# Last stage: ScalarE writes two of the input norms as scale times x plus shift

## The chip, the cores and the metric

One Trainium2 chip, one core of it. The time is the device time of the whole program in microseconds, the median of several runs. The core has four compute engines that each run their own instruction stream in order: TensorE (PE; its weight loads are shown as PEld), VectorE (DVE), ScalarE (ACT) and GpSimd (POOL). SyncE (SP) issues transfers. They wait for each other through semaphores.

## The reference, cut to what matters

A chain of four layers over x of 8 sequences x 256 tokens x 128 features, each layer a token mixer and a feed-forward part, each with a norm ahead and one behind. Only the last layer matters here. Its mixer's scores are over channels (b, k, q), its feed-forward part routes each token to two of eight experts by its distance to their centroids.

```python
def _layernorm(x, axis=-1, eps=1e-05):
    m = jnp.mean(x, axis=axis, keepdims=True)
    v = jnp.var(x, axis=axis, keepdims=True)
    return (x - m) / jnp.sqrt(v + eps)
...
x = x + _layernorm(_L3_attn_ref(_layernorm(x, axis=-1), L3_attn_Wq, L3_attn_Wk, L3_attn_Wv, L3_attn_Wo), axis=-1)
x = x + _layernorm(_L3_ffn_ref(_layernorm(x, axis=-1), L3_ffn_centroid, L3_ffn_Wg, L3_ffn_bg, L3_ffn_W1, L3_ffn_b1, L3_ffn_W2, L3_ffn_b2), axis=-1)
```

The change is in how the two inner `_layernorm(x)` of these two lines are written: the one ahead of the mixer and the one ahead of the router and experts.

## The kernel before

The last stage is one call of `experts` with `by_distance` true. x lies in SBUF as 16 tiles of 128 tokens by 128 features; a run is four tiles (two sequences), so there are four runs, 0 to 3. Both parts of the layer are in the same stage: its opening does mixer and router for the four runs, interleaved, then come the expert blocks (slots, in pairs of gate/up and down matmuls) and a tail with the last norm.

`mixed_events` is one list of events, written by hand. Every engine walks the same list and does its own part of each event, in order, with no reordering; an engine that must wait at one event does nothing of a later one. Step k of the list takes, with a = k, b = k-1, c = k-2, d = k-3: `c_shift c`, `c_res c`, `c_scores b`, `c_proj a`, `stats c`, `one_hot d`, `c_zn b`, `gap d`, `norm c`, then spot and share of d (the ranks of the chosen experts and the row places), the sends, `c_stats a+1`, `c_out b`, `router c`, `c_norm a+1`, `score c`. The events that start with c_ are the mixer's.

What each engine does at the events around the change:

- `c_norm r` (mixer's input norm). VectorE: `channel_norm`, four writes by `centred` (L1810) into `cy`, (x - mean) * rstd, after GpSimd's power operation (L1714) made rstd. TensorE: fillers, then four transposes (L2412). ScalarE: one copy of them to `cyT` (L2188).
- `c_proj r`. TensorE: q/k (L2274) and v (L2279). ScalarE: copies (L2191, L2196).
- `c_scores r`. TensorE: scores (L2293). VectorE: adds the block mask and takes the maximum (L1837 on). ScalarE: Exp.
- `c_zn r`. VectorE scales the weights, TensorE multiplies by v (L2305), ScalarE copies (L2209).
- `c_out r`. TensorE: output projection (L2313). VectorE: its statistics (L1798).
- `c_shift r`, `c_res r`. VectorE makes a shift (L1857), ScalarE writes the output norm as scale times projection plus shift (`normed`, L2145), VectorE adds it to x (L2083).
- `norm r` (the router's input norm). VectorE: four writes by `centred` into `yrow` (L1810). TensorE: fillers, four transposes (L2435). ScalarE: copy to `yT` (L2219), then a second copy of the rows (L2222).
- `router r`, `score r`. TensorE: the products with the centroids (L2446). VectorE: distances, the two best experts.
- `gap r`: Exp on ScalarE (L2228). `spot r`: TensorE ranks the choices (L2329, L2334).

Between these, the experts' weights are cut into high and low parts: VectorE subtracts the last row (L1815), ScalarE writes the high part (L2137 to L2139), VectorE the low part (L1822 to L1824). `keep_busy` puts filler matmuls (L2267) into TensorE's queue, a fixed number at each place; TensorE runs through them before it takes up what follows. The router's rows go to DRAM by GpSimd's indirect transfers (L1726), four tiles x two copies a run, and the expert blocks are loaded from there. The first slot comes after the ranks of run 3.

Of the kernel before, what the change touches and what calls it, by code (L numbers as in the profile page):

```python
# [14 lines left out]
ALU = mybir.AluOpType  # L15
# [3 lines left out]
P = 128  # L19
# [3 lines left out]
TILES = SEQS * T  # L23
# [12 lines left out]
RT = 4  # L36
# [1478 lines left out]
def experts(nc, g, layer, key, w, mix=None, out=None):  # L1515
# [8 lines left out]
    by_distance = layer == 3  # L1524
# [8 lines left out]
    x = g.x  # L1533
    rows, acc = g.rows[layer], g.acc[layer]
    with ExitStack() as ctx:
        st = Stage(nc, ctx, f"m{layer}")
# [47 lines left out]
        if by_distance:  # L1584
            cat = columns(g.w[mix], MIX)
            dist = [st.sb(f"dist{k}", [P, RT, 2]) for k in range(2)]
            shares = st.sb("shares", [P, 2, RT])
            sq_y = st.sb("sq_y", [P, TILES])
            ones_f = st.sb("ones_f", [P, P])
            c2 = st.sb("c2", [P, 3 * NE])  # L1590
            flat = [p[:, :, :, :].rearrange("p k t d -> p (k t d)") for p in parts]
            cqk = [p.rearrange("p (t c) -> p t c", t=RT) for p in flat[0:2]]
            cvT = [flat[2][:, k * RUN:(k + 1) * RUN] for k in range(2)]
            cy, cyT = flat[3][:, 0:RUN], flat[3][:, RUN:2 * RUN]
            ccT, cf = (st.sb(n, [P, RUN]) for n in ("ccT", "cf"))
            cz, cz_exp, czn = (st.sb(n, [P, 2, P]) for n in ("cz", "cz_exp", "czn"))
            ctop, cneg, ctotal, crecip = (st.sb(n, [P, 2]) for n in ("ctop", "cneg", "ctotal", "crecip"))
            cshift = st.sb("cshift", [P, TILES])

        loaded = g.loaded[key]  # L1600
        (tables_ready, places_ready, region_ready, hi_ready, split_ready, in_var, in_rstd, y_ready, copied, yT_ps,
# [14 lines left out]
        result_sent = [st.sem(f"result_sent{k}") for k in range(RB)]  # L1616
        parts_loaded = [st.sem(f"parts_loaded{r}") for r in range(RUNS)]
        if by_distance:
            dist_ready, c2_ready, c2_ps, less_ready, stored = (st.sem(n) for n in (
                "dist_ready", "c2_ready", "c2_ps", "less_ready", "stored"))  # L1620
            (c_in_var, c_in_rstd, c_y_ready, c_yT_ps, c_yT_ready, c_qk_ps, c_qk_ready, c_v_ps, c_v_ready, c_z_ps,
             c_top_ready, c_exp_ready, c_zn_ready, c_cx_ps, c_cx_ready, c_out_ps, c_out_var, c_out_rstd, c_shift_ready,
             c_f_ready, c_x_done) = (st.sem(n) for n in (
                 "c_in_var", "c_in_rstd", "c_y_ready", "c_yT_ps", "c_yT_ready", "c_qk_ps", "c_qk_ready", "c_v_ps",
                 "c_v_ready", "c_z_ps", "c_top_ready", "c_exp_ready", "c_zn_ready", "c_cx_ps", "c_cx_ready", "c_out_ps",
                 "c_out_var", "c_out_rstd", "c_shift_ready", "c_f_ready", "c_x_done"))
# [39 lines left out]
        def tiles(r):  # L1666
            return slice(r * RT, r * RT + RT)
# [100 lines left out]
        def _(dve):  # L1768
# [39 lines left out]
            def centred(k, j, r, o):  # L1808
                t = r * RT + j
                return nc.vector.tensor_scalar(o, x[:, t, :], mv[k][:, t, 0:1], rstd[k][:, t:t + 1], ALU.subtract, ALU.mult)  # L1810
# [6 lines left out]
            def split(e):  # L1817
# [6 lines left out]
                nc.vector.tensor_tensor(down[0:r, 2, 1, :], raw_rest, down[0:r, 2, 0, :].bitcast(F32),  # L1824
                                        ALU.subtract).then_inc(split_ready, 1)

            def channel_norm(r):
                dve.wait_ge(c_in_rstd, r + 1)
                if r >= 1:
                    dve.wait_ge(c_yT_ps, r)  # L1830
                for j in range(RT):
                    last = centred("c_in", j, r, cy[:, j * P:(j + 1) * P])
                last.then_inc(c_y_ready, 1)

            def channel_scores(r):
                dve.wait_ge(c_z_ps, r + 1)
# [15 lines left out]
                    last = nc.vector.tensor_scalar(czn[:, s, :], cz_exp[:, s, :], crecip[:, s:s + 1], None, ALU.mult)  # L1852
                last.then_inc(c_zn_ready, 1)

            def shifts(k, r, o, ready, done):
                dve.wait_ge(ready, r + 1)
                nc.vector.scalar_tensor_tensor(o[:, tiles(r)], mv[k][:, tiles(r), 0], -1.0, rstd[k][:, tiles(r)],  # L1857
                                               ALU.mult, ALU.mult).then_inc(done, 1)

            def norm(r):  # L1860
                dve.wait_ge(in_rstd, r + 1)
                for j in range(RT):
                    last = centred("in", j, r, yrow[0][:, r * RT + j, 0:P])
                last.then_inc(y_ready, 1)
# [263 lines left out]
        def _(act):  # L2128
# [53 lines left out]

            for kind, r, *_ in events:
                if kind == "c_norm":
                    act.wait_ge(c_yT_ps, r + 1)
                    if r >= 1:
                        act.wait_ge(c_v_ps, r)
                    nc.scalar.activation(cyT[:, :], ps[:, 0, :], ACT.Copy).then_inc(c_yT_ready, 1)  # L2188
# [21 lines left out]
                if kind == "c_shift":  # L2210
                    if r >= 1:
                        act.wait_ge(c_x_done, r)
                    normed(r, c_shift_ready, c_f_ready, lambda j: cf[:, j * P:(j + 1) * P],
                           lambda j: ps[:, 6, j * P:(j + 1) * P], "c_out", cshift)
                if kind == "norm":
                    act.wait_ge(yT_ps, r + 1)
                    if r >= 2:
                        act.wait_ge(router_ps, r - 1)
                    nc.scalar.activation(yT[r % 2][:, :], ps[:, 7, :], ACT.Copy).then_inc(yT_ready, 1)  # L2219
                    act.wait_ge(y_ready, r + 1)  # L2220
                    n = P - 1 if by_distance else P
                    nc.scalar.activation(yrow[1][:, tiles(r), 0:n], yrow[0][:, tiles(r), 0:n], ACT.Copy).then_inc(copied, 1)  # L2222
# [1368 lines left out]
```

## Time and profile before

| what | value |
|---|---|
| median of 3 runs | 1065.38 us (1065.27 to 1066.95) |
| the profiled execution | 1067.32 us |
| its span, first to last instruction | 1065.6 us |
| mean granted TensorE clock | 0.957 |
| PE busy | 941.6 us (88%) |
| DVE busy | 731.4 us (69%) |
| ACT busy | 561.7 us (53%) |
| POOL busy | 471.6 us (44%) |
| the opening of the last stage | 860 to 945 us |
| its first expert slot | 951.3 us |

The shares are means over stages with different limits. A row of the timeline gives the start, the length, the engine, the line, the operation with the names it writes and reads, how many instructions were merged, and in square brackets the idle time of the engine just before and what ended it. m_parts holds the mixer's `cy` and `cyT` among others, m_yrow the router's rows, m_banks all of PSUM.

### The profile page before, as it was taken

Reading aid. Unit: us, or ns where it says so; the run is one execution under the profiler, and the core shown is the slowest. Engines: PE = TensorE matmul, PEld = TensorE weight load, DVE = VectorE, ACT = ScalarE, POOL = GpSimd, SP = SyncE. Lnnn points to the kernel's source line nnn. Section 1 sums busy time; section 2 is a strip of 40 time slices with the busy share of each in tenths; the row PEclk is TensorE's granted clock in tenths of the full one; section 3 lists DMA queues with packets and bytes.
Section 4 is the critical chain, followed back from the end, with each engine's and each line's share of the span. In section 5 each row is a group of like instructions: output and inputs, shape, how many; then the busy total and the mean of one; then the engine's idle time right before and its main releaser. Section 6 shows DMA issues by size and latency. Waiting matters only on the chain. (4 is left out here: it accounts for less than half of the span.)

```text
span 1065.6 us, 24404 instructions
## 1 busy us (share of the span) xinstructions
PE 941.6 (88%) x8310; PEld 740.4 (69%) x8310; DVE 731.4 (69%) x2014; ACT 561.7 (53%) x1168; POOL 471.6 (44%) x528
## 2 busy tenths in 40 slices
PE   7999987999994799999979999999999968869990
PEld 6666665889993676665666666777666857869990
DVE  4677754676665678888567567676577778866664
ACT  2567673246663467777536555544445435326662
POOL 2366655464345222232454333343456432685442
PEclk9999999899997899999989999999999988999995
DMA  9211120022113024222210011110111720022214
GB/s 307 63 55 54 56 66 11 25 73 67 40 49 88 1 63 132 73 69 73 71 31 2 3 42 42 42 41 3 42 42 42 273 71 1 27 66 72 61 39 118
DMA packets 80739, 66.47 MB, mean 62 GB/s; under 512 B 6690, under 2 KB 73425, under 8 KB 80235
## 3 DMA queue, kind: packets, MB, share of 16 engines
q1 hardware_dynamic: 71883, 54.34, 18.2%
q0 software_dynamic: 4512, 8.47, 2.4%
q10 hardware_dynamic: 4224, 2.10, 0.8%
q8 instruction: 71, 1.16, 0.5%
q14 instruction: 49, 0.40, 0.1%
HBM read 38.76 MB, written 26.58 MB: 61 GB/s over the span
## 5 line engine op out<-in xcount | busy, mean ns | idle before, releaser
L780 DVE TENSOR_REDUCE a_rowmax<-a_banks 128x4 f32<-128x1024 f32 (+1 forms) x112 | 136.9, 1223 | 49.9 <-PE a_banks L1147 19.7
L2662 POOL TENSOR_TENSOR a_both<-a_probs 128x512 f32<-128x512 f32 x64 | 86.5, 1351 | 141.7 <-ACT a_probs L2964 141.6
L964 ACT ACTIVATE a_probs<-a_banks 128x1024 f32<-128x1024 f32 x112 | 114.8, 1025 | 53.8 <-PE a_banks L1128 42.6
L1733 POOL DMA_INDIRECT acc<-m_result,m_yb x77 | 75.4, 980 | 89.6 <-DVE m_result L2045 49.8
L2964 ACT ACTIVATE a_probs<-a_banks 128x1024 f32<-128x1024 f32 x64 | 65.5, 1023 | 85.5 <-PE a_banks L3136 85.5
L2818 DVE TENSOR_REDUCE a_rowmax<-a_banks 128x4 f32<-128x1024 f32 x64 | 77.7, 1220 | 12.5 <-PE a_banks L3109 12.5
L1726 POOL DMA_INDIRECT rows<-m_yrow,m_idx x64 | 65.3, 1020 | 38.5 <-issue 18.6
L2158 ACT ACTIVATE m_gate<-m_banks 128x352 f32<-128x352 f32 (+1 forms) x93 | 42.8, 460 | 65.9 <-PE m_banks L2364 65.9
L3152 PE MATMUL a_banks<-a_probs,a_V 128*64 128x256 f32 x512 | 69.4, 392 | 0.0
L655 POOL TENSOR_SCALAR_AFFINE_SELECT a_probs<-a_probs 128x512 f32<-128x512 f32 (+1 forms) x48 | 37.9, 790 | 63.3 <-ACT a_probs L964 63.2
L2390 PE MATMUL m_banks<-e_down,m_hT_hi 128*128 (+2 forms) x231 | 64.2, 346 | 0.6 <-DVE m_hT_lo L2028 0.6
L1170 PE MATMUL a_banks<-a_probs,a_V 128*32 128x256 f32 x720 | 58.0, 394 | 0.5 <-POOL a_probs L655 0.4
L2267 PE MATMUL m_banks<-ident 128*128 128x128 f32 x362 | 52.6, 308 | 2.4 <-DVE m_score L1881 1.5
L2362 PE MATMUL m_banks<-e_gu_hi,m_y_hi 128*128 x154 | 53.9, 350 | 0.4 <-issue 0.4
L1128 PE MATMUL a_banks<-a_QT,a_KT 25*128 25x256 f32 x384 | 48.1, 325 | 6.5 <-DVE a_rowmax L780 5.2
L2028 DVE TENSOR_TENSOR m_hT_lo<-m_banks,m_hT_hi 128x384 fp32r<-128x384 f32 x93 | 51.1, 549 | 3.6 <-ACT m_hT_hi L2164 3.6
L2022 DVE TENSOR_TENSOR m_h<-m_banks,m_gate 128x342 f32<-128x342 f32 (+1 forms) x55 | 28.5, 518 | 36.2 <-ACT m_gate L2158 36.2
L2267 PEld LDWEIGHTS m_banks<-ident 128*128 128x128 f32 x362 | 50.0, 221 | 4.0 <-issue 2.8
L2391 PE MATMUL m_banks<-e_down,m_hT_lo 128*128 (+2 forms) x231 | 51.7, 224 | 0.0
L2364 PE MATMUL m_banks<-e_gu_hi,m_y_lo 128*128 x154 | 49.7, 323 | 0.0
L2375 PE MATMUL m_banks<-ident,m_h 128*128 128x128 f32 (+2 forms) x279 | 47.3, 279 | 2.7 <-DVE m_hT_lo L2028 2.3
L2363 PE MATMUL m_banks<-e_gu_lo,m_y_hi 128*128 x154 | 49.5, 321 | 0.0
(403 smaller groups left out, 2764.5 us busy)
## 6 DMA issues: line engine op xcount, KB each, us to landing
rows<-fill SPq DMA_DIRECT2D x16, 520.0 KB, 4.3
a_factor<-recip_rows SPq DMA_DIRECT2D x28, 256.0 KB, 4.7
rows<-fill SPq DMA_DIRECT2D x15, 455.0 KB, 3.9
m_yb<-rows SPq DMA_DIRECT2D x77, 65.0 KB
a_expert<-in_experts SPq DMA_DIRECT2D x16, 257.5 KB
e_gu_lo<-in_gu SPq DMA_DIRECT2D x1, 2736.0 KB
e_last_row<-in_last_rows SPq DMA_DIRECT2D x1, 2736.0 KB
e_gu_lo<-in_gu SPq DMA_DIRECT2D x1, 2464.0 KB, 12.0
```

Of the source, the lines that this page charges most:

```text
L780: nc.vector.reduce_max(o, src, AX).then_inc(rowmax_ready, 1)
L964: nc.scalar.activation(probs[h][:, k, :, :], ps[:, 4:6, :], ACT.Exp, scale=SCALE).then_inc(exp_done, 1)
L1170: last = mm(o[:, 0:SEQ], v, probs[h][:, b // 2 + (0 if causal else 2 * kt), jj, (b % 2) * SEQ:(b % 2 + 1) * SEQ], start=kt == 0, stop=kt = ...
L1726: nc.gpsimd.indirect_dma_start(rows.rearrange("n p c -> (n p) c"), bass.IndirectOffsetOnAxis(idx[:, c:c + 1], 0), yrow[k][:, r * RT + t, : ...
L1733: nc.gpsimd.indirect_dma_start(acc.rearrange("k n d -> (k n) d"), bass.IndirectOffsetOnAxis(yb[b % YB][:, P:P + 1].bitcast(U32), 0), resul ...
L2267: mm(ps[:, b, 0:P], g.ident[:, :], g.ident[:, :], start=True, stop=True)
L2362: mm(o, y_hi[i % 3][:, :], gu_hi[:, s], start=True, stop=False)
L2390: mm(both, hT_hi[i % 2][0:r, c, :], part[0:r, c, :, :], start=c == 0, stop=False)
L2662: nc.gpsimd.tensor_tensor(both[u % 4][:, :, :], p[:, :, 0, :], p[:, :, 1, :], ALU.add).then_inc(both_ready, 1)
L2818: nc.vector.reduce_max(rowmax[i % 2][:, :, j, :, n].rearrange("p t h -> p h t"), ps[:, b:b + 2, :].rearrange("p h (t k) -> p h t k", t=T), ...
L2964: nc.scalar.activation(probs[u % 4][:, :, :, :].rearrange("p h t q -> p h (t q)"), ps[:, 4:6, :], ACT.Exp, scale=SCALE).then_inc(exp_done, 1)
L3152: last = mm(ps[h * D64:(h + 1) * D64, 6, 0:SEQ], V[i % 3][:, kt, j, :], probs[b][:, h, kt, :], start=kt == 0, stop=kt == T - 1)
```

## The change

In the last stage alone, VectorE no longer writes the two input norms. For each run it makes one shift per token, minus mean times rstd (`shifts`, one operation over 128 x 4), and ScalarE writes the four tiles as rstd * x + shift with `normed`. ScalarE does this at the same event of the list, ahead of its copy of the transposes, and so behind all that stands before that event in its own order. The transposes wait for ScalarE's write in place of VectorE's. The first stage with the same code (`by_distance` false) keeps its norm on VectorE.

```diff
--- before.py
+++ after.py
@@ -1595,7 +1595,7 @@
             ccT, cf = (st.sb(n, [P, RUN]) for n in ("ccT", "cf"))
             cz, cz_exp, czn = (st.sb(n, [P, 2, P]) for n in ("cz", "cz_exp", "czn"))
             ctop, cneg, ctotal, crecip = (st.sb(n, [P, 2]) for n in ("ctop", "cneg", "ctotal", "crecip"))
-            cshift = st.sb("cshift", [P, TILES])
+            cshift, c_in_shift, in_shift = (st.sb(n, [P, TILES]) for n in ("cshift", "c_in_shift", "in_shift"))
 
         loaded = g.loaded[key]
         (tables_ready, places_ready, region_ready, hi_ready, split_ready, in_var, in_rstd, y_ready, copied, yT_ps,
@@ -1616,6 +1616,7 @@
         result_sent = [st.sem(f"result_sent{k}") for k in range(RB)]
         parts_loaded = [st.sem(f"parts_loaded{r}") for r in range(RUNS)]
         if by_distance:
+            c_in_shift_ready, in_shift_ready = st.sem("c_in_shift_ready"), st.sem("in_shift_ready")
             dist_ready, c2_ready, c2_ps, less_ready, stored = (st.sem(n) for n in (
                 "dist_ready", "c2_ready", "c2_ps", "less_ready", "stored"))
             (c_in_var, c_in_rstd, c_y_ready, c_yT_ps, c_yT_ready, c_qk_ps, c_qk_ready, c_v_ps, c_v_ready, c_z_ps,
@@ -1824,13 +1825,13 @@
                 nc.vector.tensor_tensor(down[0:r, 2, 1, :], raw_rest, down[0:r, 2, 0, :].bitcast(F32),
                                         ALU.subtract).then_inc(split_ready, 1)
 
+            def shifts(k, r, o, ready, done):
+                dve.wait_ge(ready, r + 1)
+                nc.vector.scalar_tensor_tensor(o[:, tiles(r)], mv[k][:, tiles(r), 0], -1.0, rstd[k][:, tiles(r)],
+                                               ALU.mult, ALU.mult).then_inc(done, 1)
+
             def channel_norm(r):
-                dve.wait_ge(c_in_rstd, r + 1)
-                if r >= 1:
-                    dve.wait_ge(c_yT_ps, r)
-                for j in range(RT):
-                    last = centred("c_in", j, r, cy[:, j * P:(j + 1) * P])
-                last.then_inc(c_y_ready, 1)
+                shifts("c_in", r, c_in_shift, c_in_rstd, c_in_shift_ready)
 
             def channel_scores(r):
                 dve.wait_ge(c_z_ps, r + 1)
@@ -1852,12 +1853,10 @@
                     last = nc.vector.tensor_scalar(czn[:, s, :], cz_exp[:, s, :], crecip[:, s:s + 1], None, ALU.mult)
                 last.then_inc(c_zn_ready, 1)
 
-            def shifts(k, r, o, ready, done):
-                dve.wait_ge(ready, r + 1)
-                nc.vector.scalar_tensor_tensor(o[:, tiles(r)], mv[k][:, tiles(r), 0], -1.0, rstd[k][:, tiles(r)],
-                                               ALU.mult, ALU.mult).then_inc(done, 1)
-
             def norm(r):
+                if by_distance:
+                    shifts("in", r, in_shift, in_rstd, in_shift_ready)
+                    return
                 dve.wait_ge(in_rstd, r + 1)
                 for j in range(RT):
                     last = centred("in", j, r, yrow[0][:, r * RT + j, 0:P])
@@ -2182,6 +2181,10 @@
 
             for kind, r, *_ in events:
                 if kind == "c_norm":
+                    if r >= 1:
+                        act.wait_ge(c_yT_ps, r)
+                    normed(r, c_in_shift_ready, c_y_ready, lambda j: cy[:, j * P:(j + 1) * P],
+                           lambda j: x[:, r * RT + j, :], "c_in", c_in_shift)
                     act.wait_ge(c_yT_ps, r + 1)
                     if r >= 1:
                         act.wait_ge(c_v_ps, r)
@@ -2213,6 +2216,9 @@
                     normed(r, c_shift_ready, c_f_ready, lambda j: cf[:, j * P:(j + 1) * P],
                            lambda j: ps[:, 6, j * P:(j + 1) * P], "c_out", cshift)
                 if kind == "norm":
+                    if by_distance:
+                        normed(r, in_shift_ready, y_ready, lambda j: yrow[0][:, r * RT + j, 0:P],
+                               lambda j: x[:, r * RT + j, :], "in", in_shift)
                     act.wait_ge(yT_ps, r + 1)
                     if r >= 2:
                         act.wait_ge(router_ps, r - 1)
```

## Rows read from the trace of the kernel before

**Rows 1.** Busy us by stretch: PE, PEld, DVE, ACT, POOL (instructions), clock, DMA.
```profile
860.00:945.00 85.00, 67.27 (x443) 60.22 (x444) 67.92 (x333) 35.20 (x84) 40.34 (x38) 0.89 0.05 17
```

**Rows 2.** Groups by shape, VectorE, 860 to 945 us: busy, mean ns.
```profile
L1810 DVE TENSOR_SCALAR m_yrow<-x,m_in_mv,m_in_rstd 128x128 f32<-128x128 f32 x16 | 4.7, 354 | 3.9 <-POOL m_in_rstd L1714 3.9
...
L1810 DVE TENSOR_SCALAR m_parts<-x,m_c_in_mv,m_c_in_rstd 128x128 f32<-128x128 f32 x16 | 4.5, 344 | 0.9 <-POOL m_c_in_rstd L1714 0.9
```

**Rows 3.** Timeline (start us, us, engine, line): ScalarE's norm; its hand-over.
```profile
1057.73 3.31 ACT L2145 ACTIVATE m_parts<-m_parts,m_shift,m_out_rstd 128x128 f32<-128x128 f32 x8 [1.26 <-DVE m_shift L1857]
...
914.42 0.16 DVE L1857 SCALAR_TENSOR_TENSOR m_cshift<-m_c_out_mv,m_c_out_rstd 128x4 f32<-128x4 f32 x1
...
914.68 1.51 ACT L2145 ACTIVATE m_cf<-m_banks,m_cshift,m_c_out_rstd 128x128 f32<-128x128 f32 x4 [3.93 <-DVE m_cshift L1857]
```

**Rows 4.** Timeline: mixer's norm, runs 0 and 1.
```profile
865.08 1.11 DVE L1810 TENSOR_SCALAR m_parts<-x,m_c_in_mv,m_c_in_rstd 128x128 f32<-128x128 f32 x4
...
866.11 0.17 DVE L1784 CAST m_limit_f<-m_limit 128x16 f32<-128x16 int32 x1
...
866.25 0.66 PE L2412 MATMUL m_banks<-ident,m_parts 128*128 128x128 f32 x4 [0.57 <-DVE m_parts L1810]
...
869.01 0.77 ACT L2137 ACTIVATE e_gu_hi<-e_gu_lo 128x684 fp32r<-128x684 f32 x1 [0.31 <-DVE e_gu_lo L1815]
...
871.07 0.63 PE L2412 MATMUL m_banks<-ident,m_parts 128*128 128x128 f32 x4 [0.63 <-DVE m_parts L1810]
...
871.10 0.58 ACT L2196 ACTIVATE m_parts<-m_banks 128x512 f32<-128x512 f32 x1
...
871.53 1.06 PE L2293 MATMUL m_banks<-m_parts 128*128 128x128 f32 x8
...
874.25 0.41 DVE L1837 TENSOR_TENSOR m_cz<-m_banks,late_w_att 128x256 f32<-128x256 f32 x1
```

**Rows 5.** Timeline: mixer's norm, run 2.
```profile
882.34 1.12 DVE L1810 TENSOR_SCALAR m_parts<-x,m_c_in_mv,m_c_in_rstd 128x128 f32<-128x128 f32 x4
...
883.51 0.66 PE L2412 MATMUL m_banks<-ident,m_parts 128*128 128x128 f32 x4
...
886.30 0.68 DVE L2083 TENSOR_TENSOR x<-x,m_cf 128x512 f32<-128x512 f32 x1
```

**Rows 6.** Timeline: router's norm, run 0.
```profile
892.18 0.60 ACT L2209 ACTIVATE m_ccT<-m_banks 128x512 f32<-128x512 f32 x1 [1.78 <-PE m_banks L2305]
...
892.44 0.95 PE L2435 MATMUL m_banks<-ident,m_yrow 128*128 128x128 f32 x4 [0.29 <-DVE m_yrow L1810]
...
893.18 1.92 PE L2313 MATMUL m_banks<-late_w_att,m_ccT 128*128 128x128 f32 x8
...
895.13 0.89 DVE L1798 BATCH_NORM_STATS2 m_c_out_stats<-m_banks 128x6 f32<-128x128 f32 x4 [1.24 <-PE m_banks L2313]
```

**Rows 7.** Timeline: TensorE's fillers and VectorE's norm, mixer, run 3.
```profile
896.45 2.91 PE L2267 MATMUL m_banks<-ident 128*128 128x128 f32 x12
...
896.67 1.12 DVE L1810 TENSOR_SCALAR m_parts<-x,m_c_in_mv,m_c_in_rstd 128x128 f32<-128x128 f32 x4
```

**Rows 8.** Timeline: router's norm, run 1.
```profile
907.79 0.60 ACT L2209 ACTIVATE m_ccT<-m_banks 128x512 f32<-128x512 f32 x1 [1.70 <-PE m_banks L2305]
...
907.82 0.63 PE L2435 MATMUL m_banks<-ident,m_yrow 128*128 128x128 f32 x4
...
908.29 0.20 ACT L2228 ACTIVATE m_th<-m_gap 128x4 f32<-128x4 f32 x1
...
908.49 1.14 PE L2313 MATMUL m_banks<-late_w_att,m_ccT 128*128 128x128 f32 x8
```

**Rows 9.** Timeline: router's norm, run 2.
```profile
924.91 0.66 PE L2435 MATMUL m_banks<-ident,m_yrow 128*128 128x128 f32 x4 [0.38 <-DVE m_yrow L1810]
```

**Rows 10.** Timeline: TensorE behind the router's norm, run 3.
```profile
943.84 3.82 PE L2267 MATMUL m_banks<-ident 128*128 128x128 f32 x32
...
948.00 0.20 PE L2329 MATMUL m_banks<-m_one_hot,m_upper 128*128 128x64 bf16 x1 [0.34 <-DVE m_chosen L1924]
```


## Prediction

> **What bounds the kernel now.** I read the profile in four steps. First the page: its 40 slices show a full TensorE with short dips, and the last dips before the long expert run lie where the last stage opens. Second, busy time by stretch, for the opening of that stage, 860 to 945 us [rows 1]: of 85.0 us VectorE is busy 67.9, TensorE 67.3 (much of it the filler of keep_busy), ScalarE 35.2, GpSimd 40.3. VectorE is the fullest engine and ScalarE is 60% idle, so the change looks obvious. But 68 of 85 is not full, and a share doesn't say who is late at a given wait. Third, the chain that ended last: it reaches back only into the last quarter of it, so for most of the stretch it gives no answer. So, fourth, the timeline, hand-over by hand-over. It shows a ring: VectorE writes a norm, TensorE turns it, ScalarE copies it, TensorE multiplies, VectorE reads. Every engine takes its events in one fixed order, and each of them waits somewhere in each step. For instance VectorE stood idle for 1.24 us until the output projection (L2313) of run 1 was done [rows 6]. In such a ring, latency on the path counts and engine time beside it does not.
>
> After 945 us TensorE is nearly full until the last expert block, and the tail is untouched. What the opening loses or gains therefore arrives at the end one for one.
>
> **What the change removes and adds.** Removed on VectorE: 8 groups of four writes, 16 for the mixer at 344 ns and 16 for the router at 354 ns [rows 2]. A group holds VectorE's queue for 1.03 us: it starts at 865.08 and the next operation, which waits for nothing, at 866.11 [rows 4]. Each group leaves one small operation like L1857's 0.16 us [rows 3]; as the next one can start before it ends (866.11 is 0.08 ahead of 865.08 + 1.11), it holds the queue for about 0.08. VectorE is relieved of about 0.95 us each time, 7.6 in all.
>
> Added on ScalarE: 8 groups of four. The same function already writes SBUF from SBUF in the tail, eight in 3.31 us, so 1.66 for four [rows 3]. All 8 together are 13.3 us on an engine with 50 us free. No table load is added: the stage already uses this function beside Exp.
>
> Added on the path: the hand-over. Before, from the first VectorE write to the first transpose took 1.17 us (865.08 to 866.25 [rows 4], 882.34 to 883.51 [rows 5]). After: start of the shift to start of ScalarE's group 0.26 us (914.42 to 914.68, the same pair of operations), the group 1.66, and about 0.05 to TensorE: 1.97. **So each hand-over is 0.80 us longer even when ScalarE stands free.** Where it isn't free, the group stands behind what ScalarE has ahead of it in its order, and that was not so before, because VectorE wrote beside it.
>
> **The eight places, in order of time** (each number is how much later the thing named starts than before; the page's own clock levels are kept).
>
> Mixer, run 0: ScalarE is free. First transpose 866.25 becomes 867.05, +0.80 [rows 4].
>
> Mixer, run 1: ScalarE's order puts two weight conversions, the q/k copy and the v copy ahead. Before, conversion 1 idled 0.31 us for VectorE [rows 4]; VectorE is now 0.95 early there, so this gives back 0.4 of the 0.8: the 0.31 and the 0.1 by which ScalarE's operations overlap when none waits (907.79 + 0.60 is 908.39, the next starts at 908.29 [rows 8]). The q/k copy moves by that 0.4, the v copy from 871.10 to 871.5, and the group can start behind its 0.58 us, at 872.0, only. It ends at 873.7, so the transposes go from 871.07 to 873.7, +2.65. The score matmuls follow 0.46 later and take 1.06 (from 871.53): done at 875.25. VectorE read them at 874.25, because it was busy till then; now it waits and reads at 875.3. **Of 2.65 the cover swallows 1.6; +1.05 stays.**
>
> Mixer, run 2: VectorE's writes at 882.34 lay under a wait for GpSimd's power operation, so removing them gains nothing. ScalarE is free. The transposes move by 1.05 + 0.80 = 1.85 (883.51), and with them the copy, the output norm and VectorE's residual add at 886.30 [rows 5], which had almost no slack: **+1.8**.
>
> Router, run 0: on ScalarE the group stands behind the copy of L2209, which itself waits for TensorE: 892.18 + 1.8 = 894.0, 0.60 long [rows 6]. Group 894.5 to 896.2. Transposes from 892.44 to 896.2: **+3.8**. In TensorE's order the output projection (L2313) stands behind these transposes, and VectorE was already idle for it (895.13 [rows 6]); so VectorE is late by 3.8 too. This is the added wait that costs most: queued behind it on TensorE are the projection and the router, on VectorE the output statistics and everything after.
>
> Mixer, run 3: TensorE runs 12 filler matmuls before these transposes, 2.91 us from 896.45 [rows 7]. Shifted by 3.8 they end at 903.2. VectorE's write stood 1.54 behind the start of the statistics (895.13 to 896.67 [rows 6, 7]), so the shift comes at 898.9 + 1.5 = 900.4 and the group ends at 902.4. Hidden: +0. Without the filler it would cost up to its 2 us.
>
> Router, run 1: the same as run 0, with the Exp of the gap ahead too. L2209's copy 907.79 + 3.8 = 911.6, Exp 908.29 + 3.8 = 912.1 (0.20 long); group 912.2 to 913.9. Transposes 907.82 to 913.9: **+6.1** [rows 8]. The ranks, the projection and the router follow on TensorE, and GpSimd's sends follow on VectorE's shares.
>
> Router, run 2: ScalarE is free, +0.80: the transposes at 924.91 [rows 9] are late by **+6.9**, and the ranks right behind them. VectorE reads those as soon as they are done.
>
> Router, run 3: again +0.80, so +7.7. Behind them TensorE has 32 fillers, 943.84 + 7.7 + 3.82 = 955.4, and only then the ranks, which began at 948.00 after 0.34 us of waiting for VectorE [rows 10]: **+7.4**. VectorE's one-hots are ready by then.
>
> The sum, as what each place adds to the lateness (run 0 of the mixer is inside run 1's figure, and at the last place the fillers swallow 0.3 of 0.8): 1.05 + 0.75 + 2.0 + 0 + 2.3 + 0.8 + 0.5 = 7.4 us. It hangs on the order of ScalarE's queue at two places (4.3 of it) and on the hand-over at the others.
>
> **TensorE's clock.** It is the one price that the trace brackets only. The projection of L2313 takes 1.92 us while the granted clock is at the lower of its two levels, 1.2 GHz (893.18) [rows 6], and 1.14 at the higher, 2.4 (908.49) [rows 8], 0.78 apart. New TensorE waits of over 2 us arise before the transposes of mixer run 1 and router runs 0 and 1; at router run 0 the clock is low already. Bounds: nothing, or one more fall at both others, with transposes, projection and ranks slow and some filler running over the next wait, about 3. Below nothing is excluded, since the waits only grow. I take 0.4, half of one projection, nearer to nothing because filler and waits further on absorb part. The Trainium skill (Perfetto Trace Analysis, Matmul Optimizations) says that TensorE scales power by utilization, so matmuls should run back to back in batches; by it alone the upper end would hold and the time be about 1076.
>
> **Against the runs.** The profiled execution took 1067.3 us, of which its span is 1065.6; the median of the runs is 1065.4, 1.9 below it. The difference is carried over: 1065.4 + 7.4 + 0.4 = 1073.2 us, and a profile after with a span near 1073.4.
>
> **The rivals.**
> VectorE is the bound: the opening shrinks by all that VectorE is relieved of, 8 x 0.95 = 7.6, to 1057.8. It decides if at each step VectorE, not TensorE, is the last to arrive; it speaks for it that VectorE has the largest share, against it the 1.24 us wait at 895.13 and that the cost moves to an engine standing on the same ring. The Trainium skill (Perfetto Trace Analysis, Optimizing Scalar/DVE Operations) says that offloading from VectorE to ScalarE may make sense if VectorE is saturated; at 68 of 85 us the trace doesn't show it saturated. Chance 0.04.
> Both cancel: every hand-over costs 0.80 but VectorE's 0.95 is paid back before the next read, and ScalarE reaches each group in time. 8 x (0.80 - 0.95) = -1.2, so 1064.2, no difference. It needs ScalarE's copy at 892.18 to be early, and the trace shows it waiting for TensorE. Chance 0.05.
> The clock falls at both new waits: +3 instead of +0.4, 1075.8. Chance 0.14.
> That the change doesn't do what it says: VectorE's eight groups would still be in the trace; nothing in the diff leaves them. Under 0.01.
>
> **How the numbers follow.** The forecast has 0.77, and 1073.2 is its value. Its own range is 1069 (the two queue places cost half, because ScalarE gets through faster or VectorE's lead helps an earlier read) to 1076. With the clock rival the range is 1069 to 1077; it leaves out the two rivals on the other side and the ends, under 2 in 10. A measurement of this kernel can tell about 0.2%, 2.1 us, from no change: faster 0.04, same 0.05, slower 0.91.
>
> **What would show it.** In the profile after, the transposes of L2435's router run 0 start about 3.8 us later, run 1 about 6.1, and ScalarE's new groups start right behind the copy of L2209. VectorE's idle before the output statistics of run 1 rises from 1.24 to over 4 us. The first expert slot begins 7 to 8 us later, and from there to the end nothing changes. VectorE's busy time in the stretch falls to about 60 us, ScalarE's rises to about 48. It would be wrong if the read at 874.25 or at 895.13 didn't move, or if VectorE's waits didn't grow.

## The result and the profile after

The kernel with the change took 1076.94 us in the median of 6 runs (1073.71 to 1089.31), the kernel before beside it 1066.04. The ratio is 1.0121, 95% interval 1.0096 to 1.0147: some 13 us slower, where 7.8 were forecast. The sign and the place were right, the size was too small. The median as it stands lies inside the range of 1069 to 1077, near its end; scaled to the median of before from which the forecast was made (1065.38) it is 1078.3, just above it. Executions that took over 1.5% longer than the fastest of the same kernel are left out of every ratio here.

The page after, busy time by engine (before: PE 941.6, DVE 731.4, ACT 561.7):

```profile
PE 942.7 (88%) x8310; PEld 741.7 (69%) x8310; DVE 723.7 (68%) x1990; ACT 575.2 (54%) x1200; POOL 470.3 (44%) x528
```

VectorE lost 7.7 us of work and ScalarE gained 13.5, as summed (7.6 and 13.3). The page says nothing of the loss: the shares moved as intended.

The profiled execution after took 1073.71 us with a span of 1072.0, only 6.4 more than before. That hides a chance difference: its last stage began 5.4 us earlier, in code that the change doesn't touch. So from here on I count from a mark inside the stage, VectorE's first subtraction of a last row (L1815 before, 864.29; L1816 after, 858.88), and call the time from there to the first gate matmul of the first slot the opening. It is this row before and this row after (from, length, then busy time of PE, PEld, DVE, ACT, POOL, then the granted clock):

```profile
864.29:951.34 87.05, 68.93 (x478) 61.18 (x477) 69.52 (x344) 34.47 (x85) 43.88 (x38) 0.92 0.07 20
```

```profile
858.88:957.49 98.61, 74.44 (x479) 65.94 (x478) 61.97 (x320) 47.47 (x117) 44.22 (x39) 0.84 0.07 19
```

87.05 us became 98.61, 11.6 more. From the first slot to the end both took the same (114.3 and 114.5), so the whole loss is in the opening, and the granted clock there fell from 0.92 to 0.84.

The timeline after, at the places of the prediction (start us, length us, engine, line; in brackets the idle time ahead and what ended it):

```profile
858.88 0.87 DVE L1816 TENSOR_TENSOR e_gu_lo<-e_gu_lo,e_last_row 128x684 f32<-128x684 f32 x1 [1.02 <-DMA e_down<-in_down]
...
859.66 0.16 DVE L1830 SCALAR_TENSOR_TENSOR m_c_in_shift<-m_c_in_mv,m_c_in_rstd 128x4 f32<-128x4 f32 x1
...
859.86 1.65 ACT L2144 ACTIVATE m_parts<-x,m_c_in_shift,m_c_in_rstd 128x128 f32<-128x128 f32 x4 [3.79 <-DVE m_c_in_shift L1830]
...
861.56 0.66 PE L2418 MATMUL m_banks<-ident,m_parts 128*128 128x128 f32 x4 [1.18 <-ACT m_parts L2144]
...
862.90 3.19 PE L2280 MATMUL m_banks<-late_w_att,m_parts 128*128 128x256 f32 x8 [0.69 <-ACT m_parts L2191]
...
869.75 0.63 PE L2418 MATMUL m_banks<-ident,m_parts 128*128 128x128 f32 x4 [2.31 <-ACT m_parts L2144]
...
872.02 0.42 DVE L1838 TENSOR_TENSOR m_cz<-m_banks,late_w_att 128x256 f32<-128x256 f32 x1 [4.48 <-PE m_banks L2299]
...
881.75 0.65 PE L2418 MATMUL m_banks<-ident,m_parts 128*128 128x128 f32 x4 [1.73 <-ACT m_parts L2144]
...
889.45 0.16 DVE L1830 SCALAR_TENSOR_TENSOR m_in_shift<-m_in_mv,m_in_rstd 128x4 f32<-128x4 f32 x1 [0.31 <-POOL m_in_rstd L1715]
...
890.37 0.60 ACT L2212 ACTIVATE m_ccT<-m_banks 128x512 f32<-128x512 f32 x1 [1.78 <-PE m_banks L2311]
...
890.86 1.64 ACT L2144 ACTIVATE m_yrow<-x,m_in_shift,m_in_rstd 128x128 f32<-128x128 f32 x4
...
892.55 1.12 PE L2441 MATMUL m_banks<-ident,m_yrow 128*128 128x128 f32 x4 [2.22 <-ACT m_yrow L2144]
...
893.46 1.92 PE L2319 MATMUL m_banks<-late_w_att,m_ccT 128*128 128x128 f32 x8
...
895.41 0.89 DVE L1799 BATCH_NORM_STATS2 m_c_out_stats<-m_banks 128x6 f32<-128x128 f32 x4 [4.28 <-PE m_banks L2319]
...
908.66 0.60 ACT L2212 ACTIVATE m_ccT<-m_banks 128x512 f32<-128x512 f32 x1 [1.99 <-PE m_banks L2311]
...
909.25 1.64 ACT L2144 ACTIVATE m_yrow<-x,m_in_shift,m_in_rstd 128x128 f32<-128x128 f32 x4
...
911.03 1.09 PE L2441 MATMUL m_banks<-ident,m_yrow 128*128 128x128 f32 x4 [2.41 <-ACT m_yrow L2144]
...
946.52 0.66 PE L2441 MATMUL m_banks<-ident,m_yrow 128*128 128x128 f32 x4 [0.87 <-ACT m_yrow L2144]
...
948.78 5.44 PE L2273 MATMUL m_banks<-ident 128*128 128x128 f32 x32
...
957.49 0.42 PE L2368 MATMUL m_banks<-e_gu_hi,m_y_hi 128*128 x1 [0.51 <-issue]
```

Read it beside [rows 4] to [rows 10]. The hand-over at mixer run 0 is shift 859.66, group 859.86, 1.65 long, transposes 861.56: 1.90 us against 1.17. At router run 0 the shift is there at 889.45, but ScalarE takes L2212's copy (L2209 before) at 890.37 and the group only behind it at 890.86; TensorE idles 2.22 us for it, and VectorE idles 4.28 us ahead of the output statistics where it idled 1.24 [rows 6]. Run 1 repeats that (908.66, 909.25, 911.03). These are the mechanisms forecast. Not forecast are the lengths on TensorE. L2280 takes 3.19 at mixer run 0, where before, behind the same wait of 0.69, it was (L2274 there):

```profile
867.59 1.99 PE L2274 MATMUL m_banks<-late_w_att,m_parts 128*128 128x256 f32 x8 [0.69 <-ACT m_parts L2188]
```

The granted clock over these eight matmuls was 1.00 before and 0.60 after. And the 32 fillers of L2273 take 5.44 where they took 3.82 [rows 10], at 0.69 in place of 1.00.

All marks counted from the first subtraction, as lateness against the first profile of before, in us; "again" is a second profile of the changed kernel (e5, below), "before again" a second profile of the kernel before (e12, below):

| what starts | forecast | after | again | before again |
|---|---|---|---|---|
| mixer run 0, transposes | 0.80 | 0.72 | 0.71 | -0.01 |
| mixer run 1, transposes | 2.65 | 4.09 | 2.59 | 0.00 |
| VectorE's read of the scores, run 0 | 1.05 | 3.18 | 0.96 | 0.01 |
| mixer run 2, transposes | 1.85 | 3.65 | 0.96 | 0.15 |
| router run 0, transposes | 3.8 | 5.52 | 2.83 | 0.15 |
| output statistics, run 1 | 3.8 | 5.69 | 3.00 | 0.32 |
| router run 1, transposes | 6.1 | 8.62 | 6.04 | 0.19 |
| router run 2, transposes | 6.9 | 9.70 | 7.13 | 1.05 |
| router run 3, transposes | 7.7 | 10.34 | 7.78 | 1.86 |
| first slot | 7.4 | 11.55 | 11.14 | 1.35 |

The last column says how far a single profile can be trusted: the kernel before repeats itself within 0.35 us up to router run 1, and at router run 3 only within 1.9.

### The profile page after: what moved, and what is told of

Same layout as the page of the kernel before. It is cut to its first block and busy times, and to the rows that moved or that the text cites. A ratio compares the mean times of both kernels' runs of the same rounds, so it can differ in the third digit from the quotient of the medians.

```text
span 1072.0 us, 24412 instructions
## 1 busy us (share of the span) xinstructions
PE 942.7 (88%) x8310; PEld 741.7 (69%) x8310; DVE 723.7 (68%) x1990; ACT 575.2 (54%) x1200; POOL 470.3 (44%) x528
## 3 DMA queue, kind: packets, MB, share of 16 engines
q8 instruction: 71, 1.16, 0.5%
## 5 line engine op out<-in xcount | busy, mean ns | idle before, releaser
L1734 POOL DMA_INDIRECT acc<-m_result,m_yb x77 | 75.5, 980 | 91.3 <-DVE m_result L2044 49.8
L2273 PE MATMUL m_banks<-ident 128*128 128x128 f32 x362 | 51.6, 303 | 2.5 <-DVE m_score L1880 1.7
L2273 PEld LDWEIGHTS m_banks<-ident 128*128 128x128 f32 x362 | 48.7, 216 | 4.4 <-issue 3.2
L1092 PE MATMUL a_banks<-ident 128*128 128x128 f32 x298 | 43.0, 288 | 7.8 <-DMA w_att<-in_att 6.4
```

What stands on the lines that cost most here:

```text
L1734: nc.gpsimd.indirect_dma_start(acc.rearrange("k n d -> (k n) d"), bass.IndirectOffsetOnAxis(yb[b % YB][:, P:P + 1].bitcast(U32), 0), resul ...
L2273: mm(ps[:, b, 0:P], g.ident[:, :], g.ident[:, :], start=True, stop=True)
```

## The experiments

The first eight ran in two sessions (e1 to e4, then e5 to e8) in which every kernel took about 1100 us and scattered more (the kernel before 1099.6 and 1100.0 in the median); what is longer there lies mainly ahead of the last stage, whose opening began between 882 and 907 us. In the third session, e9 to e12, the kernel before took 1067.65. The record gives e1 to e4 and e9 to e12 the same chip number, so what made the first two slower is not known. I compare ratios to the kernel before in the same session, and marks inside the opening. One profile stands for one execution, and the clock is part luck, which is why e5 and e12 repeat the two kernels themselves. In four profiles of those two sessions (e1, e4, e5, e7) TensorE also idled 2.3 us between the transposes of the first two expert blocks, where the others show 0.69 (e8: 1.58, and 2.0 ahead of the first). e5 has it and the first profile after, the same kernel, has not, so it follows no edit; it puts about 2 us on the opening of these four, 1.6 of it at this place. Router run 3's transposes are the last mark ahead of it.

### One norm at a time

```diff
 # e1: the router's norm stays on VectorE
             def norm(r):
-                if by_distance:
-                    shifts("in", r, in_shift, in_rstd, in_shift_ready)
-                    return
 # e2: the mixer's norm stays on VectorE
             def channel_norm(r):
-                shifts("c_in", r, c_in_shift, c_in_rstd, c_in_shift_ready)
+                ... four writes by centred, as before
```

(and ScalarE's side of each goes with it)

> Only the mixer's input norm on ScalarE; the router's stays on VectorE. I read the opening of the last stage as the time from VectorE's first subtraction of a last row (L1815 before, L1816 after) to the first gate matmul of the first slot: before 951.34 - 864.29 = 87.05 us, after 957.49 - 858.88 = 98.61, 11.6 more. Theory path-and-clock (hand-overs 7.4 us as summed, the rest TensorE's lower clock): opening 89 to 91, that is 2 to 4 more, time 1067.5 to 1069.5. Rival clock-only (hand-overs are covered, TensorE's waits only push its clock down): most of the loss starts at mixer run 1, so 7 or more of the 11.6 should be here already, 1073 or above. Rival VectorE-bound: not slower at all, 1062 to 1065.

> Only the router's input norm on ScalarE. Theory path-and-clock: 2.0 + 2.3 + 0.8 + 0.5 = 5.6 us of hand-over and queue order plus 1 to 3 us of clock: opening 93.5 to 96, time 1072 to 1075, and the context copy (L2209 before) with the new group right behind it at router runs 0 and 1. Rival clock-only: the smaller part, under 1070. If both parts add up, this and the mixer's run give 11.6 together.

Measured: e1 1.0036 (0.9996 to 1.0077), opening 92.96; e2 1.0055 (1.0019 to 1.0091), opening 94.12. The ratios add up to 0.9%, and the changed kernel has 1.0 to 1.2%; each is known to about 0.4%, so this agrees but doesn't prove much. The openings, 5.9 and 7.1 more, add up to 13.0 against 11.6, and to 11.4 without the 1.6 us of that wait. The router's part is as expected in its opening (93.5 to 96) and just under in its time. The mixer's part is larger than expected by its opening, not by its ratio; at its own places it is as forecast (transposes of run 1 +2.59, read of the scores +0.96), and by router run 3 it is 3.1 late. Of its opening's 5.9, 2.8 arise behind that, 1.6 of them in the wait named above. Clock-only wanted 7 or more of the opening here and fails by it, and with it VectorE-bound, which wanted nothing; the ratio of e1 alone excludes neither.

### More fillers in the changed kernel

```diff
-                    keep_busy((9, 0, 8, 6)[r], 0)
+                    keep_busy((13, 8, 14, 6)[r], 0)
...
-                        keep_busy((0, 0, 7, 12)[r], 7)
+                        keep_busy((8, 9, 10, 15)[r], 7)
```

> The changed kernel with more filler matmuls ahead of the transposes that now wait for ScalarE: mixer runs 0, 1, 2 get 13, 8, 14 in place of 9, 0, 8; router runs 0 to 3 get 8, 9, 10, 15 in place of 0, 0, 7, 12. Theory path-and-clock: the granted clock stays at 2.4 GHz through more of the opening, about 4 us come back and the 7.4 us of hand-over stay: opening 94 to 96, time 1072 to 1074. Rival clock-only: nearly all 11.6 come back, 1066 to 1068. Rival latency-only (the clock costs nothing, my sum is too small): no change from the changed kernel, 1077; where the clock is low anyway the fillers take twice as long and it could be slower.

Measured: ratio 1.0059 (1.0022 to 1.0095); the unaltered changed kernel had 1.0100 (1.0058 to 1.0142) in the second session (e5). By time alone the two are not told apart. The profiled execution was the longest of its twelve, 1122.52 us, with an opening that shows nothing of it:

```profile
907.18:999.85 92.67, 74.17 (x561) 66.92 (x560) 62.17 (x320) 47.15 (x117) 44.40 (x38) 0.97 0.06 19
```

92.67 us, a little under the expected 94 to 96, at a granted clock of 0.97. Against 98.61 this gives back 5.9 by doing more on TensorE; against e5 without the waits at the first blocks (96.0, below) it is 3.3. What is left over before is 5.6 by a profile in which the clock was held; the kernel before held it at 0.92 only. The output projection of run 1 (L2319) took 1.06 us here against 1.92 before and after. The read of the scores is late by 1.17 (forecast 1.05), router run 3 by 5.47. **With the clock held 5.6 us of loss stay, and 3.3 to 5.9 us go.** That what goes is the clock and nothing else rests on the lengths of TensorE's rows, not on a time measured beside the changed kernel.

### ScalarE's order

```diff
                 if kind == "c_zn":
+                    if r >= 1:
+                        q = r - 1
+                        normed(q, in_shift_ready, y_ready, lambda j: yrow[0][:, q * RT + j, 0:P],
+                               lambda j: x[:, q * RT + j, :], "in", in_shift)
                     act.wait_ge(c_cx_ps, r + 1)
```

(and `norm` on ScalarE writes run 3 only)

> The changed kernel, but in ScalarE's order the router's norm of runs 0 to 2 stands ahead of the context copy and not behind it. Theory path-and-clock: at runs 0 and 1 the transposes come 1.2 and 1.9 us earlier (the hand-over of 1.97 us alone is left), some 1 us of clock with it: opening 94.5 to 96, time 1073 to 1074.5. Rival that ScalarE's queue order is not what makes it late: no change, 1077.

Measured: ratio 1.0045 (1.0005 to 1.0084), opening 96.71, a little over the expected 94.5 to 96. Up to mixer run 2 its marks equal the changed kernel's within 0.15 us, low clock included, so this pair is the cleanest of the study: router run 0's transposes come 1.2 us earlier (4.31 late for 5.52), run 1's 4.1 earlier (4.56 for 8.62) where the two places, at the expected 1.2 and 1.9 each, give 3.1. The rest fits the clock: between the two places the 12 fillers ahead of mixer run 3's transposes took 1.58 us (granted clock 1.00) in place of 2.91 (0.50). Router run 3 is 6.33 late in place of 10.34. The opening gained only 1.9, since the stretch behind router run 3 was 2.1 longer than in the first profile after, the wait at the first blocks. By time alone the rival of no change isn't settled, 1.0045 (up to 1.0084) against 1.0100 (from 1.0058) in another session; by the marks it falls. The queue order is what made these two places the dearest.

### The changed kernel again, and VectorE's relief taken back

> The changed kernel once more, unaltered, to see how much of the opening is luck of TensorE's clock. Opening (first VectorE subtraction of a last row to first gate matmul of the first slot) was 98.6 us against 87.1 before. Theory path-and-clock: the hand-over part (about 7.4 with the clock pattern of before, 5.6 with the clock held) comes again; the rest, 4, moves with the granted clock: opening 95 to 99. Rival latency-only: 98.6 within 0.3 again.

Measured: ratio 1.0100 (1.0058 to 1.0142), opening 98.20. The opening alone would look like the rival; the marks don't. In this execution the clock didn't fall at mixer run 0:

```profile
900.80 1.99 PE L2280 MATMUL m_banks<-late_w_att,m_parts 128*128 128x256 f32 x8 [0.69 <-ACT m_parts L2191]
...
906.15 0.63 PE L2418 MATMUL m_banks<-ident,m_parts 128*128 128x128 f32 x4 [2.50 <-ACT m_parts L2144]
...
907.70 0.42 DVE L1838 TENSOR_TENSOR m_cz<-m_banks,late_w_att 128x256 f32<-128x256 f32 x1 [2.26 <-PE m_banks L2299]
```

L2280's eight matmuls took 1.99 us (granted clock 1.00), not 3.19 (0.60), the transposes of mixer run 1 started 9.37 us after the mark (906.15 - 896.78), not 10.87, and the read of the scores was 0.96 late, not 3.18. From there to router run 3 the marks lie within 1 us of the forecast and end on it, 7.78 for 7.7. Then the fillers were slow again:

```profile
984.27 5.30 PE L2273 MATMUL m_banks<-ident 128*128 128x128 f32 x32
```

That is 5.30 for 3.82, at a granted clock of 0.71. From the first rank matmul to the first slot it took another 2.2 us more than before, in the waits at the first two blocks. Without those this opening is 96.0, so the kernel's two profiles lie 2.6 us apart, as they do at router run 3: the rival falls.

```diff
                 nc.vector.scalar_tensor_tensor(o[:, tiles(r)], mv[k][:, tiles(r), 0], -1.0, rstd[k][:, tiles(r)],
                                                ALU.mult, ALU.mult).then_inc(done, 1)
+                if by_distance and k in ("in", "c_in"):
+                    for j in range(RT):
+                        centred(k, j, r, dead[:, j * P:(j + 1) * P])
```

> The changed kernel, and VectorE writes the same four tiles after each shift into a buffer that nobody reads: its 7.6 us of relief are taken back, the path is the changed one. Theory path-and-clock: the relief was worth nothing beyond 0.4 at mixer run 1, so the opening stays that of the changed kernel, 96 to 100, within what the clock moves. Rival VectorE-bound: 7 us more than the changed kernel, 103 or above.

Measured: ratio 1.0083 (1.0039 to 1.0127), against 1.0100 without the dead writes. Opening:

```profile
888.42:990.57 102.15, 75.62 (x478) 66.91 (x478) 70.28 (x351) 47.43 (x117) 45.66 (x40) 0.82 0.07 21
```

VectorE's work is back (70.28 us busy for 61.97) and the marks are those of the first profile after: router run 3 late by 10.16 for 10.34, the score read of run 3 by 9.18 for 9.44. Up to there the relief bought nothing at all. The opening as a whole is 102.15, above the expected 96 to 100 and just short of the rival's 103; it is 3.5 more than in the first profile after, all of it behind router run 3; its fillers took 5.14, and TensorE then idled 2.0 us ahead of the first block. That part varies from execution to execution, so I don't lay it to the dead writes; nor is it excluded that some of it is theirs. The ratio says that the time is not 7 us more, as VectorE-bound wanted.

### Can the kernel before be had faster by the same reasoning

```diff
-                keep_busy((0, 4, 4, 0)[r], 5)
+                keep_busy((6, 12, 12, 0)[r], 5)
```

> The kernel before, with nothing of the change, and more filler matmuls only: ahead of the mixer's value products 6, 12, 12, 0 in place of 0, 4, 4, 0. The run with fillers in the changed kernel had the clock at 1.00 through most of the opening and its output projections at 1.1 us in place of 1.9. Theory path-and-clock: the kernel before also pays for low clock at mixer run 0's and 1's projection; opening 87.1 goes to 85 to 86, time 1 to 2 us less. Rival that fillers only cost: opening 87 to 88.

Measured: ratio 1.000 (0.9966 to 1.0033), opening 87.26, what the rival wanted (87 to 88) and not the theory (85 to 86). The fillers did their work at first: the ranks of run 0 came 2.0 us earlier than before. By the residual add of run 3 only 1.0 was left and at the first slot nothing. This early gain wasn't kept.

> The changed kernel with both cures: the router's norm of runs 0 to 2 ahead of the context copy in ScalarE's order, and more fillers (mixer transposes 13, 8, 14, 6; router transposes 4, 2, 10, 15; values 6, 12, 12, 0). Fillers alone had an opening of 92.7 and order alone 96.7. Theory path-and-clock: of the 5.6 left with fillers, 1.2 + 1.5 were queue order at router runs 0 and 1; opening 89.5 to 91, still above before by the bare hand-overs (0.8 each at mixer run 2, router 0 to 3, less what is hidden). Rival that the relief of VectorE pays once the clock is cured: 87 or less.

(ScalarE's order of e4, the mixer's fillers of e3, the router's 4, 2, 10, 15, and the values' of e6.) Measured: ratio 1.0027 (0.9987 to 1.0067), opening 95.26; router run 3 is 4.87 late. By the ratio it is the best form of the whole change with whole-group hand-overs, and still not faster than before. Its opening misses the expected 89.5 to 91: behind router run 3 it lost another 3.3, of which about 2.2 is the wait at the first blocks.

### The hand-over itself

```diff
                     for j in range(RT):
+                        pe.wait_ge(y_ready, RT * r + j + 1)
                         last = nc.tensor.transpose(ps[:, 7, j * P:(j + 1) * P], yrow[0][:, r * RT + j, 0:P], g.ident[:, :])
```

(and each of the four writes signals; the same for the mixer; the second copy of the rows waits for four times as many. e9 on the kernel before, e10 on the changed one.)

> The kernel before, VectorE writing both norms, but it signals after each tile and each of the four transposes waits for its own tile only; no engine does more or less. Marks count from VectorE's first subtraction of a last row. Theory path-and-clock (latency of the hand-over is what counts): the last transpose ends about 0.45 us earlier at each place, the transposes of router run 3 move from 77.3 to 74.5 or 75.5, time 1.5 to 2.5 us less. Rival that these hand-overs are covered and only the clock counts: 77.3, no change in time.

Measured: **ratio 0.9976 (0.9958 to 0.9994)**, 2.6 us less than before, with the same instructions. Opening 85.88; before in the same session (e12) 88.41, in the first profile 87.05. The residual add of run 3 comes 1.4 and 2.6 us earlier than in these two. Against the first profile alone the expected mark (74.5 to 75.5) was missed, at 76.58; against the one of the same session (79.16) it is 2.6 earlier, as the time is. That agreement is in part luck: in e9 the output projection of run 0 took 1.16 us and in both profiles of before about 2, which is 0.8 us of it, and e2 and e6 had the 1.16 without this edit; and the two profiled executions themselves took 1064.95 (e9) and 1064.23 us (e12). The gain rests on the ratio, 12 executions against 23. One more caution holds for e9 and e10: with a signal for each tile the first of four transposes starts sooner, while the last may not, so that the start of a group is an early mark. The residual adds behind it are free of this.

> The changed kernel with the same signal by tile. ScalarE's group of four lasts 1.65 us with one every 0.4, so three of four transposes leave the path: 0.45 us back at each of seven places. Theory path-and-clock: transposes of router run 3 at 82 to 85 (87.6 and 85.1 in the two profiles without), time 3 us less than the changed kernel. Rival: 85 to 88.

Measured: ratio 1.0051 (1.0033 to 1.0069), opening 92.18, router run 3 at 82.18. That is 5 to 7 us less than the changed kernel by ratio, where 3 were expected. At the copy behind the transposes of router run 3, which needs all four tiles, it is 2.2 and 4.7 us earlier than the two profiles of the changed kernel. How much of it is the hand-over and how much the clock (0.87 over the opening, for 0.84 and 0.86) is not separated. e9 and e10 also make the cleanest measurement of the change itself, both sides with signals by tile and in one session: 1.0051 / 0.9976 is 1.0075, 8 us, to about 3 us either way.

(In e11 the router's norm is VectorE's again, and so are the mixer's runs 0 and 1.)

```diff
+                if r < 2:
+                    ... four writes by centred on VectorE, as before
...
-                    if r >= 1:
+                    if r >= 2:
                         act.wait_ge(c_yT_ps, r)
-                    normed(r, c_in_shift_ready, ...
+                        normed(r, c_in_shift_ready, ...
```

> Only the mixer's runs 2 and 3 on ScalarE, where it stands free or TensorE's fillers cover it; all else on VectorE, as before. This measures one bare hand-over. Theory: the mixer's transposes of run 2 come 0.80 us later than before (19.22 to 20.0) and the router's of run 0 too (28.15 to 28.95); run 3 adds nothing beyond that. Rival that VectorE's relief of 0.95 us pays it back there: the router's transposes of run 0 at 28.1 or less.

Measured: ratio 1.0019 (0.9993 to 1.0046), opening 88.88. The transposes of mixer run 2 started 20.13 us after the mark and the router's of run 0 at 29.01: late by 0.91 and 0.86, of which 0.2 stood there already from the kept shifts. So a bare hand-over costs 0.7 to 0.8 us, as forecast, and the relief of 0.95 doesn't pay it back at that place. At router run 1 the lateness is 0.38: run 3's norm, under the fillers, cost nothing.

> The kernel before once more, unaltered, for its profile on this chip. The opening of 87.1 us and the marks (mixer 1.96, 6.78, 19.22, 34.86; router 28.15, 43.53, 60.62, 77.30) stand on one profiled execution. Theory path-and-clock: within 1 us of them, since VectorE's writes keep TensorE's waits short; the changed kernel's two profiles lay 2.6 us apart.

Measured: opening 88.41, 1.35 more than the first, and router run 3 1.86 later: more than the expected 1 us. Up to router run 1 all marks but one lie within 0.35 us of the first profile; between the score read of run 3 and the residual add of run 3 it lost 1.0, at the same place where e1, e6 and e11 lost about 1. What decides that is open; it lies where GpSimd's transfers are.

## Why the prediction was wrong

**The path was right; how closely its sum fits is in part luck.** In the second profile, where the clock didn't fall at mixer run 0, router run 3 is 7.78 late for a forecast 7.7, and each place ahead within 1 us. The terms: the bare hand-over 0.72 for 0.80 (0.7 to 0.8 in e11); mixer run 1 2.59 for 2.65, of which 0.96 stays for 1.05; the queue place at router run 0 2.1 (3.00 at the output statistics less 0.89 at the residual add ahead) for 2.0; router run 1's 3.0 (6.04 - 3.00) for 2.3, low clock included; mixer run 3 hidden, for hidden; router run 2 1.1 and router run 3 0.65, for 0.8 each. Mixer run 2 is 0.9 less than forecast, and 0.77 of that is no effect of the change: the output projection ahead of it took 1.16 us in place of 1.94, and it did so too in e2, whose mixer is the one of before. This chance and router run 1's excess cancel. Against the second profile of before (e12) the same mark would be 5.9 late, so the 7.7 is borne out to about 2 us, not to 0.1.

**VectorE's relief was worth nothing, and its one term had the wrong reason.** At mixer run 1 I let it give back 0.4 us. In e8, with the relief taken back, ScalarE's second conversion started 5.04 us after the mark and in the changed kernel 5.03: ScalarE comes 0.72 late to it by the hand-over itself and finds VectorE's subtraction done either way. The 0.4 is there, but as cover of the hand-over; router run 3 moved by -0.2 us (e8).

**The step that failed is the paragraph on TensorE's clock, the term of 0.4 us in the sum.** It took half of one slow projection, with an upper bound of about 3. The runs showed 2.1 to 4.2 in the first profile and, at the first slot, 1.5 in the second. In the first profile the lateness exceeds the forecast by 2.1 us at the first read of the scores (projections of 3.19 for 1.99, the scores behind them 1.77 for 1.06), by 1.9 at the output statistics of run 1, by 2.6 at router run 3 and by 4.15 at the first slot; the last step is the 32 fillers, behind which the ranks are 11.47 late where the transposes were 10.34 and I had let 0.3 go. In the second it is -0.1, -0.8, 0.1 and 3.7, or 1.5 without the waits at the first blocks: the fillers again. Two profiles of the changed kernel, alike but for the clock at mixer run 0 (0.60 and 1.00), lie 2.6 us apart from there on. Three errors made it small. I looked for the price at the projection behind each new wait and not at the work ahead of mixer run 1's transposes, where the first fall was. I counted fillers as cover that absorbs a fall; but where the ranks stand behind a fixed number of them, as at router run 3, a slow filler is itself on the path. And I gave the fall even odds at one place, where the waits had grown at most of them. Holding the clock (e3) brought the opening back by 5.9 against the first profile, more than the excess of 4.15. It also held it where the kernel before had it low, at the output projections of runs 0 and 1 (1.16 and 1.06 us for 1.94 and 1.92), which is 1.6 us and fits.

**The upper end was bounded by one mechanism.** The rival with more clock stood at 1075.8 with a chance of 0.14; what came was that rival and some more. The range would have had to reach to 1079. Part of what came is not laid to the clock either: of the second profile's lateness at the first slot, 2.2 us are the waits at the first two blocks.

**What stays open:** why the clock falls at mixer run 0 in some executions and not in others of the same kernel; what the wait at the first two blocks is in the two slower sessions (the unaltered kernel before has no profile there); and the 1 us that some executions lose where GpSimd's sends run.

## What to carry to other kernels

In a ring of engines that hand tiles to each other, move work by the latency of the hand-over and by the receiver's queue order, not by busy shares: moving 7.6 us off the fullest engine cost 13, and putting them back on it moved nothing up to router run 3. Ask of each move what stands ahead of the work in the new engine's order, and what stands behind the consumer on its own. If the hand-over is what counts, shorten it first: a signal for each tile in place of one for four made the kernel before 0.24% faster (0.06 to 0.42) with no instruction moved.

## What the runs showed of the hardware that I had not expected

- The same kernel runs the same eight projection matmuls in 1.99 or in 3.19 us (granted clock 1.00 and 0.60), after the same wait of 0.69 us, in different executions. The wait ahead of the transposes before it was nearly the same too, 1.07 and 1.18 us. In e4 and e8, where nothing up to that place differs on the path, they took 3.32 and 2.84. So a single profile can't price a wait.
- A filler meant to keep the clock up costs more when it fails: the same 32 matmuls took 3.82 us at a granted clock of 1.00 (before, e1, e2, e3) and 5.44, 5.30, 5.45 and 5.14 at 0.69 to 0.73 (both profiles of the changed kernel, e4, e8).
- VectorE can be given 8.3 us more work in the opening (61.97 to 70.28 us busy) with no mark up to router run 3 moving by over 0.3 us (first profile after against e8).
